# Attention with cross-context and feed-forward in one kernel: the row of negated maxima turned by VectorE and placed by four DMAs, and attention outputs in two PSUM banks

## The reference

```
z   = layernorm(x)
q   = z @ Wq.T                     # 16 heads of 96
k,v = [z; ctx] @ Wk.T, Wv.T        # 4 key/value heads of 96, 576 keys
s   = q k^T / sqrt(96)             # per head 512 x 576
x1  = x + softmax(s) v @ Wo.T
out = x1 + layernorm(relu(z1 @ up)^2 @ down + ((z1 @ fc1 @ expert) * sum(top2(z1 @ gate))) @ fc2),  z1 = layernorm(x1)
```

## Time and profile before

| | |
|---|---|
| median of 3 runs | 2142.66 us (2142.64 to 2143.2) |
| the profiled execution: its own time | 2143.96 us |
| its span | 2142.1 us |
| PE busy | 2115.3 us (99%) |
| DVE busy | 793.8 us (37%) |
| ACT busy | 695.1 us (32%) |
| POOL busy | 752.5 us (35%) |
| chain that ended last, PE's share | 92% |

### The profile page before, as it was taken

One profiled execution on the slowest core, in us unless ns is written; L12 is line 12 of the kernel. 1 busy time (PEld: TensorE's weight loads), 2 busy tenths in 40 slices (PEclk: granted clock), 3 DMA queues, 4 the chain that ended last, 5 costly groups with the idle time before them and its releaser, 6 DMA issues.

```text
span 2142.1 us, 30395 instructions
## 1 busy us (share of the span) xinstructions
PE 2115.3 (99%) x9724; PEld 1740.6 (81%) x9724; DVE 793.8 (37%) x1401; ACT 695.1 (32%) x1206; POOL 752.5 (35%) x616
## 2 busy tenths in 40 slices
PE   8999999999999999999999999999999999999998
PEld 7888888877777777878888878787878888888886
DVE  4231312278787777841100313222221232222222
ACT  5111211167777777751111223211123321111111
POOL 2533030146776776662212433010014422222221
PEclk9999999999999999999999999999999999999999
DMA  6743433635655655534334344222124532222222
GB/s 196 263 147 137 167 118 99 174 81 134 164 135 135 162 144 125 142 101 146 134 126 153 128 144 156 103 73 88 64 79 135 192 113 83 86 76 89 79 90 70
DMA packets 231517, 269.51 MB, mean 126 GB/s; under 512 B 77456, under 2 KB 145296, under 8 KB 230544
## 3 DMA queue, kind: packets, MB, share of 16 engines
q1 hardware_dynamic: 186592, 196.58, 29.8%
q10 hardware_dynamic: 44848, 71.97, 10.9%
HBM read 175.93 MB, written 92.29 MB: 125 GB/s over the span
## 4 chain that ended last, share of the span: by engine, by line
PE 92%; DMA 3%; DVE 2%; POOL 1%; issue 1%; ACT 1%; SPq 0%; ACTq 0%; DVEq 0%; POOLq 0%
PE psum L117 28%; PE psum L118 28%; PE psum L119 28%; PE psum L968 4%; DMA staging<-in_up_w 2%; POOL operands L1261 1%; PE psum L231 1%; PE psum L1019 1%; PE psum L1020 1%; PE psum L1003 1%; PE psum L1002 1%; DVE operands L539 0%; ACT operands L1256 0%; PE psum L975 0%; DMA staging<-in_x 0%
## 5 line engine op out<-in xcount | busy, mean ns | idle before, releaser
L117 PE MATMUL psum<-operands 128*128 128x512 f32 (+3 forms) x2888 | 1122.5, 389 | 13.8 <-DVE operands L351 9.8
L118 PE MATMUL psum<-operands 128*128 128x512 f32 (+3 forms) x2888 | 1110.5, 385 | 0.0
L119 PE MATMUL psum<-operands 128*128 128x512 f32 (+3 forms) x2888 | 1109.0, 384 | 0.0
L117 PEld LDWEIGHTS psum<-operands 128*128 128x128 f32 (+1 forms) x2888 | 543.7, 188 | 121.0 <-DVE operands L351 9.2
L119 PEld LDWEIGHTS psum<-operands 128*128 128x128 f32 (+1 forms) x2888 | 544.1, 188 | 106.5
L118 PEld LDWEIGHTS psum<-operands 128*128 128x128 f32 (+1 forms) x2888 | 544.8, 189 | 93.8
L1261 POOL TENSOR_TENSOR operands<-staging,operands 128x512 fp32r<-128x512 f32 x92 | 118.2, 1296 | 368.0 <-ACT operands L1256 367.5
L1147 DVE TENSOR_REDUCE small<-psum 128x1 f32<-128x576 f32 x256 | 192.1, 750 | 100.0 <-PE psum L968 100.0
L1860 POOL TENSOR_TENSOR operands<-operands 128x640 fp32r<-128x640 f32 x64 | 100.0, 1568 | 319.4 <-ACT operands L1855 319.2
L889 POOL TENSOR_TENSOR operands<-staging,operands 128x512 fp32r<-128x512 f32 x128 | 164.1, 1290 | 35.6 <-ACT operands L1069 26.7
L1712 DVE TENSOR_TENSOR staging<-staging 128x512 f32<-128x512 f32 x64 | 45.3, 726 | 307.0 <-ACT staging L1678 306.2
(11 more groups left out here) (112 smaller groups left out, 1318.5 us busy)
## 6 DMA issues: line engine op xcount, KB each, us to landing
h_scratch<-staging ACTq DMA_DIRECT2D x80, 256.0 KB, 2.2
operands<-h_scratch SPq DMA_DIRECT2D x64, 320.0 KB, 3.1
operands<-recip_scratch SPq DMA_DIRECT2D x64, 192.0 KB, 4.2
o_scratch<-staging SPq DMA_DIRECT2D x64, 192.0 KB, 4.9
operands<-o_scratch SPq DMA_DIRECT2D x64, 192.0 KB, 2.8
operands<-q_hi_scratch ACTq DMA_DIRECT2D x14, 768.0 KB, 5.9
operands<-q_lo_scratch ACTq DMA_DIRECT2D x14, 768.0 KB, 5.9
staging<-in_x SPq DMA_DIRECT2D x20, 512.0 KB, 3.9
```

Of the source, the lines that this page charges most:

```text
L117: e.matmul(o, lh, rh, start=first, stop=False)
L118: e.matmul(o, lh, rl, start=False, stop=False)
L119: return e.matmul(o, ll, rh, start=False, stop=last)
```

## The change

Four things are changed.

1. Turning. PE's transpose, `b_pe_row`, is gone. `nm` becomes a tile of 128 x 32 (zeroed once by the new memset of 128 x 64), of which the reductions fill four columns, and DVE's transpose turns it in four blocks of 32 x 32. The result `nmT` has, in partitions 32k to 32k+3, the maxima of queries 32k to 32k+31 of each of the four query tiles.
2. Placing. `row_in` issues four DMAs for a head instead of one, each of 4 pieces of 32 numbers. Each raises its semaphore by 16, so the waits on `b_row` ask for 64.
3. Place on DVE. `b_dve_row` stands inside `split` of slot 3, between the copy and the subtraction, instead of behind both. It waits for its own maxima instead of for PE.
4. Banks. The output of an odd head is added up in bank 6, that of an even head in bank 2, which the turned row has left; `pv` waits for the copy out of the head before last. Stage c's second tile, which uses bank 2, waits for the last copy out.

```diff
         def a_dve(e):
+            e.memset(sm[:, 88:152], 0.0)
...
-        rowst = [mmf(VB + 4 * NT * VW + r * P, P, ST) for r in range(2)]
-        nm = [sm[:, 80 + ST * r:80 + ST * (r + 1)] for r in range(2)]
+        nm = [sm[:, 88 + 32 * r:120 + 32 * r].bitcast(f32r) for r in range(2)]
+        nmT = [sm[:, a:a + 32].bitcast(f32r) for a in (152, 200)]
...
+        def o_bank(o):
+            return PS[:, 6 if o % 2 else 2, :]
...
-                e.dma_start(raw(qp[p][0][HD:HD + 1, a * S:(a + 1) * S]).rearrange("o (u s) -> o u s", u=ST),
-                            raw(rowst[r])).then_inc(b_row[r], 16)
+                for k in range(P // 32):
+                    e.dma_start(raw(qp[p][0][HD:HD + 1, a * S:(a + 1) * S]).rearrange("o (u k s) -> o u k s", u=ST, s=32)[:, :, k, :],
+                                raw(nmT[r][32 * k:32 * k + ST, :])).then_inc(b_row[r], 16)
...
-        def b_pe_row(e, i, o):
-            e.wait_ge(*past(b_mx, head(i, o) * ST + ST))
-            e.wait_ge(*past(b_rw, head(i, o)))
-            e.transpose(PS[0:ST, 2, 0:P], nm[o % 2], ident[:]).then_inc(b_rt, 1)
...
-                    e.wait_ge(*past(b_row[o % 2], 16 * nth(i, o, 2) + 16))
+                    e.wait_ge(*past(b_row[o % 2], 64 * nth(i, o, 2) + 64))
...
-                    e.wait_ge(*past(b_oe, head(i, o)))
+                    e.wait_ge(*past(b_oe, head(i, o) - 1))
...
-                    parts3(e, PS[:, 6, :], v0, v1, pt[j][0], pt[j][1], j == 0, False).then_inc(b_pt, 1)
+                    parts3(e, o_bank(o), v0, v1, pt[j][0], pt[j][1], j == 0, False).then_inc(b_pt, 1)
...
-            e.wait_ge(*past(b_rt, head(i, o) + 1))
-            e.wait_ge(*past(b_row[o % 2], 16 * nth(i, o, 2)))
-            e.tensor_copy(rowst[o % 2], PS[0:ST, 2, 0:P]).then_inc(b_rw, 1)
+            e.wait_ge(*past(b_mx, head(i, o) * ST + ST))
+            e.wait_ge(*past(b_row[o % 2], 64 * nth(i, o, 2)))
+            e.transpose(raw(nmT[o % 2]), raw(nm[o % 2])).then_inc(b_rw, 1)
...
                 e.tensor_copy(pt[j][0], bank).then_inc(b_hid, 1)
+                if row:
+                    b_dve_row(e, i, o + 2)
                 e.wait_ge(*past(b_hid, k))
...
             for j in range(NT):
+                if j == 3:
+                    e.wait_ge(*past(b_mx, 3 * ST))
                 st(0, 0, j)
...
             def tile(b, t, transposes=False):
                 e.wait_ge(*past(cc_x1, b * ST + t - 1))
+                if b * ST + t == 1:
+                    e.wait_ge(*past(b_oe, NH))
```

More of the change, by code:

```diff
@@ L723, in xattn_ffn_kernel @@
         b_S, b_mx = sem("b_max_scores"), sem("b_max", 1)
-        b_rt, b_rw = sem("b_row_transposed", 2), sem("b_row_copied", 1)
+        b_rw = sem("b_row_turned", 2)
         b_row = [sem(f"b_row_placed{r}", 16) for r in range(2)]
@@ L730, in xattn_ffn_kernel @@
         b_pt = sem("b_pv_tile", NT)
-        b_oe, b_rcp, b_om = sem("b_o_left", 1), sem("b_recip"), sem("b_o_scaled", 2)
+        b_oe, b_rcp, b_om = sem("b_o_left", 2), sem("b_recip"), sem("b_o_scaled", 2)
         b_s4 = [sem(f"b_sums_turned{r}") for r in range(2)]
@@ L980, in b_pe_first @@
                 b_pe_max(e, 0, t - 1, k // 2, su_first)
-            if t > 1 and k == ST:
-                b_pe_row(e, 0, t - 2)
         def b_pe(e):
@@ L1016, in pv @@
                 if j < ST:
-                    parts3(e, PS[:, 6, :], v0, v1, pt[j][0], pt[j][1], j == 0, False).then_inc(b_pt, 1)
+                    parts3(e, o_bank(o), v0, v1, pt[j][0], pt[j][1], j == 0, False).then_inc(b_pt, 1)
                 else:
-                    e.matmul(PS[:, 6, :], v0, pt[j][0], start=False, stop=False)
-                    e.matmul(PS[:, 6, :], v1, pt[j][0], start=False, stop=True).then_inc(b_pt, 1)
+                    e.matmul(o_bank(o), v0, pt[j][0], start=False, stop=False)
+                    e.matmul(o_bank(o), v1, pt[j][0], start=False, stop=True).then_inc(b_pt, 1)
             def body(i, last):
@@ L1026, in body @@
                             st(i, hh + 1, j)
[L1027 to L1031, removed]
+                        if j < ST and not (last and hh + 3 >= 2 * G):
+                            b_pe_max(e, i, hh + 3, j)
                         if last and hh == 2 * G - 1 and j == 0:
@@ L1039, in b_pe @@
             e.wait_ge(*past(b_cst, 10))
-            b_pe_row(e, 0, 2)
             for j in range(NT):
+                if j == 3:
+                    e.wait_ge(*past(b_mx, 3 * ST))
                 st(0, 0, j)
@@ L1088, in out @@
                 e.wait_ge(*past(b_os[o], 16 * nth(i, o, 2 * G)))
-                e.activation(ou[o], PS[:, 6, :], ACT.Copy).then_inc(b_oe, 1)
+                e.activation(ou[o], o_bank(o), ACT.Copy).then_inc(b_oe, 1)
             def load_wo(i, q):
@@ L1144, in b_dve_max @@
             if u == 0:
-                e.wait_ge(*past(b_rt, head(i, o) - 1))
+                e.wait_ge(*past(b_rw, head(i, o) - 1))
             e.wait_ge(*past(b_S, head(i, o) * ST + u + 1))
@@ L1161, in b_dve, with split @@
         def b_dve(e):
-            def split(i, o, j):
+            def split(i, o, j, row=False):
                 t = head(i, o) * NT + j
@@ L1196, in body @@
                     if to_split:
-                        split(i, hh + 1, 3)
-                    if to_max:
-                        b_dve_row(e, i, hh + 3)
+                        split(i, hh + 1, 3, to_max)
                     if to_split:
```

## The result

The changed kernel takes 2164.71 us (median of 5 runs, 2156.03 to 2166.34), the kernel before 2142.80 (5 runs, 2142.64 to 2146.27). The ratio is 1.0088, interval 1.0066 to 1.0111. The forecast was 2128.4, so it was wrong in size and in sign. The profiled execution of the changed kernel took 2166.34 us, its span is 2164.5 us: 22.4 more than the 2142.1 of before.

The account below looks back on a forecast made before the run. PE, busy 99% of the span, was taken as the bound. The terms -8.3 - 8.8 + 1.2 + 1.3 + 0.3 = -14.3 us took the profiled 2143.96 to 2129.7, or 2128.4 us against the median; range 2124.8 to 2136.5.

Parts of the forecast that it names:

- the row in every fourth head: Row's four DMAs behind three value loads, 15 heads: 3.3 us left against a 2.0 to 3.6 landing, priced 1.2 us.
- A fixed 0.3 us: PE's scores, which need the row, were taken to be due 0.3 us sooner in the new rhythm.
- slower: the rows come late in every head: Rival at each head's first scores: fourth piece lands in 5.2 us, 0.6 us lost 62 times, 2162 us; 5%.
- Transpose, -8.3: PE loses one transpose in each of 64 heads, at 0.13 us each: -8.3 us, lower bound -1.9.
- banks, -8.8: First `pv` of 63 heads no longer waits for ACT's copy out, 0.14 us each: -8.8 us.
- banks bring nothing, 5.5 us left: Rival at the first `pv`: something else comes as late as ACT, 5.5 us gain left, 2137 us; 7%.
- DVE: DVE's transpose delays the next instruction 0.13 us; stretch from copy to next head's first reduction changes by -0.15 us; priced nothing.
- DVE takes over: Rival: second pair of maxima waits for DVE, whose transpose holds it longer; expected 2133 to 2140 us; 15%.
- Last body: Row already late behind four stage c loads; three more issues make it later: 1.3 us, between 0.6 and 2.0.
- Start: Stage's first `pv`: value loads come three issues later, behind head 1's row: 0.3 us, bounds 0 and 1.5.

Follow-up runs that it names:

- e1: Changed kernel with ACT's 768 KB query load in every fourth head cut to 64 columns of one head: 2131.91 us.
- e3: Kernel before (transpose on PE, one bank) with its row placed by four DMAs of one 512-byte piece each instead of one DMA: 2150.61 us.
- e8: Kernel before (transpose on PE, one DMA, one bank) with the same three changes to the order of loads as e6: 2144.03 us.
- e6: Changed kernel, context value loads one head sooner, stage c's first loads behind the last body's row, first value loads issued by ACT: 2126.39 us.
- e5: Changed kernel with SP's three loads of the context's values issued one head sooner, two heads ahead of the large query load: 2128.03 us.
- e4: Changed kernel with SP's three loads of the context's values issued behind the next row instead of ahead of it: 2151.77 us.
- e9: Changed kernel with ACT's large query load issued some 4 us later, behind its copy out and the fifth slot's exponential: 2154.15 us.

## Why the prediction was wrong, step by step

**The failed step** is the row in every fourth head: "3.3 us are left, against 2.0 to 3.6. At this very place the sums' transfer took 2.0", priced at 1.2 us with bounds 0 and 4.5. It measured 36.9 us, in 14 heads; the fifteenth with value loads has no large load beside it. Three things were wrong in it.

- *The landing.* 2.0 us was read at the right place, and at the wrong moment: that transfer was issued at 819.84, 1.69 us ahead of ACT's load at 821.53. The fourth piece leaves at the load's side and needs 4.87 us. Such a number stood in the prediction: 4.15 us behind stage c's loads, used only for the last body and for the rival. What was left out is the other queue: the load is issued by ACT, and only SP's queue had been read. The Trainium skill, "DMA: Bandwidth & Descriptors", section "Queues, rings and completion order", says that the queues of the issuing engines share the same 16 DMA engines in turns. e1, where only ACT's load is smaller and SP's row lands in time, agrees with the sharing; of turns the changed kernel's packets show nothing for 2.6 us (705.6 to 708.2).
- *What shifts.* The gain itself moves ACT's load nearer to the row: 2.49 us after the first issue before (2.29 to 2.59 in 11 heads of 14), 2.17 after. At the old rhythm and with four issues (e3) most heads still pass. A fixed 0.3 us was taken off PE's due time, and nothing off the load's.
- *What a late row costs.* 1.80 us late in the head shown, not 0.3, and beside the waits 10.2 us of halved clock in the heads. The clock goes with the spread of the runs: the five executions go from 2156.03 us at a mean granted clock of 0.997 to 2166.34 at 0.991. The fastest is still 13 us slower than before, and without its clock loss of some 6 us (0.3% of 2156) it would still be slower.

The trace of the kernel before held the collision once: there the transfer of the sums issued at 534.67 leaves 0.10 us ahead of ACT's load at 534.77. The prediction's 3.6 us was the larger of two windows, and not the most that this transfer takes. Its row in the window 534 to 535 us:

```profile
small<-staging SPq DMA_DIRECT2D x1, 2.0 KB, 5.7
```

The rival "slower: the rows come late in every head" had 5%. Its landing (5.2 us) and its time (2162) were near, its place was not: one head in four, at four times its 0.6 us each (36.9 / 14 = 2.6). That the time agrees is luck. It should have been asked for the heads that have the value loads and the large load, and would then have had a far larger chance.

**Transpose, -8.3, and banks, -8.8.** Right together (17.6 measured from e8 to e6, 58 heads from 7.95 to 7.67 us), wrong apart: 1.4 and 16.3 in that order. The two places of a head were read as two independent losses, though both lie in one stretch that ACT sets (1.86 us up to the first matmul of the output). The bound "banks bring nothing, 5.5 us left" was therefore wrong too: with one bank 1.4 are left. (Line 1019 is the output's last matmul but one, and not its fourth-last; the distances read there are right.)

**DVE.** 0.13 us until the next instruction, as taken; its stretch by 0.20 us shorter, not 0.15. The rival "DVE takes over" did not come: the second pair of maxima is followed at the clean 0.27 us.

**Last body.** PE's scores start 2.29 us after their place (958.97 for 956.68), before 0.16 (934.33 for 934.17; the 0.43 of the earlier trace rows is idle time of the weight loads): 2.1 where 1.3 were taken, bounds 0.6 and 2.0; yet the last five heads take 35.5 us in both kernels. **Start.** +2.4 us against 0.3, outside its bound of 1.5. The term itself was right: the first output starts at 443.45, 0.30 us later than before, behind a wait of 1.77. What came on top is the clock at its lower level from 442.9 to 449.7 (0.66 on average from 440 to 450 us, before 1.00). In e5 this wait is 1.60 us, the clock stays at 1.00, and the first head ends at 449.74, 0.6 us sooner than before.

With the failed term taken out (e5), the kernel takes 2128.03 us, where the sum had come to 2128.4. That agrees to less than the last body's miss and the start's (0.6 us sooner where 0.3 later was expected), so part of it is luck.

## What to carry to other kernels

A small transfer with a deadline is timed against the large loads of all queues, not against its own queue: lay the issues of SP and of ACT on one line of time, and see what leaves within a few tenths of a microsecond of the last piece, in the new rhythm and not in the old one. When a thing is moved out of such a collision, ask first who stands there next (e4 and e9 both passed it on). And before two gains on one engine are added, look whether another engine holds both ends of the stretch in which they lie.

## What the runs showed of the hardware

- A small transfer's time to landing depends on a few tenths of a microsecond. A row's last piece that is issued 0.36 us or more ahead of the 768 KB load isn't waited for; one issued 0.15 us ahead of it comes 4.87 us after its issue, and its packets start when the load's have run for 2.4 us (from 705.84 to 708.26). The 2 KB transfer of the sums goes from 2.0 us to 5.6 beside the load (705.39 in the changed kernel) and 5.7 (534.67 in the kernel before).
- Pieces of 128 and of 512 bytes are both late beside the load; an issue of either holds SP for some 0.6 us.
- A halved clock can come with a wait of PE, and lasted 3.4 or 6.8 us here. It began between 0.5 us before and 1.8 us after the wait's end. Waits of 1.15 to 1.81 and of 2.09 us in the changed kernel had none with them, those of 1.77, 1.87 and 2.02 had, so the wait's length alone doesn't decide.
- A transpose of 128x32 float32 in square blocks takes DVE 200 to 205 ns, and costs the next instruction 0.13 us.
